# Attention layer on one core: root operations two to a step, normalisations in one slot, joints of the stages

## What is computed

```
h = _L0_tok_ref(log_dt, x, B, inv_A_real, A_imag, 1024)      # (16, 128, 1024)
h = jnp.concatenate([h, txt], axis=1)                         # (16, 205, 1024)
h = h + _L0_attn_ref(_layernorm(h, axis=-1), Wqkv, Wo)
h = h + _L0_ffn_ref(_layernorm(h, axis=-1), base_W, base_b, router_W, router_b, A, B, expert_map)
```

## Time and profile before

| | |
|---|---|
| median of 3 timed executions | 1586.72 us (1586.7 to 1587.28) |
| profiled execution | 1590.28 us, of which the span from first to last instruction 1588.5 us |
| busy: TensorE | 1454.7 us (92% of the span) |
| busy: VectorE | 1119.1 us (70%) |
| busy: ScalarE | 743.7 us (47%) |
| busy: GpSimd | 402.1 us (25%) |
| first stage | to 154 us |
| second stage | 154 to 924 us |
| third stage | 924 us to the end |
| pairs of the second stage, by their first projection product (L733) | start at 170.13, 229.40, 318.94, 408.43, 497.97, 587.50, 677.04 and 766.53 us; the tail begins at about 852.5 us |

### The profile page before, as it was taken

How to read it: one execution, slowest core, us unless ns; L and a number is a source line. 1 busy time by engine, 2 the same in 40 slices (tenths; PEclk the granted TensorE clock), 3 DMA queues, 4 the chain that set the end, 5 groups by cost and what they waited for, 6 DMA issues and landing times. The chain is left out here.

```text
span 1588.5 us, 28828 instructions
## 1 busy us (share of the span) xinstructions
PE 1454.7 (92%) x9700; PEld 1302.3 (82%) x9700; DVE 1119.1 (70%) x4187; ACT 743.7 (47%) x2642; POOL 402.1 (25%) x289
## 2 busy tenths in 40 slices
PE   0475899999999999999998979999999999999999
PEld 0475888888888788888887769999999999999888
DVE  8999689898988989898988755444444444444464
ACT  3595287887878687887887531111111111111101
POOL 0000154444445354444444400101010000000010
PEclk9988899999999999999999999999999999999999
DMA  9846555465636455465666251212121212121211
GB/s 293 280 99 139 99 81 114 65 128 85 121 59 120 85 81 116 66 129 80 132 149 120 88 198 40 80 40 79 40 79 40 79 40 79 40 79 40 70 49 41
DMA packets 107501, 152.51 MB, mean 96 GB/s; under 512 B 9060, under 2 KB 93412, under 8 KB 106456
## 3 DMA queue, kind: packets, MB, share of 16 engines
q1 hardware_dynamic: 105752, 150.27, 40.9%
q10 hardware_dynamic: 1632, 0.79, 0.3%
HBM read 73.90 MB, written 51.38 MB: 79 GB/s over the span
## 5 line engine op out<-in xcount | busy, mean ns | idle before, releaser
L828 ACT ACTIVATE P<-P,nmax 128x128 f32<-128x128 f32 (+1 forms) x1024 | 434.3, 426 | 95.2 <-DVE nmax L926 91.7
L899 POOL TENSOR_TENSOR P<-P,rden 128x512 f32<-128x512 f32 (+1 forms) x256 | 331.8, 1318 | 402.9 <-DVE rden L932 402.6
L926 DVE CUSTOM_DVE_ANT_0 P<-sc,mask 128x128 f32<-128x128 f32 (+1 forms) x1024 | 292.4, 323 | 71.3 <-PE sc L703 66.4
L733 PE MATMUL pr<-xT_hi,wq_hi 128*128 128x410 f32 x576 | 242.7, 421 | 0.7 <-DVE xT_lo L953 0.7
L938 DVE COPY PTR<-pt 128x282 f32<-128x282 f32 x512 | 221.1, 432 | 16.5 <-PE pt L713 15.4
L1202 PE MATMUL b<-w_hi,x2T_hi 128*128 128x390 f32 (+3 forms) x624 | 214.4, 344 | 1.0 <-DVE x2T_lo L1334 1.0
L1202 PE MATMUL b<-w_lo,x2T_hi 128*128 128x390 f32 (+3 forms) x624 | 212.5, 341 | 0.0
L1202 PE MATMUL b<-w_hi,x2T_lo 128*128 128x390 f32 (+3 forms) x624 | 212.0, 340 | 0.0
L1295 POOL TENSOR_TENSOR ht<-ht 128x1024 f32<-128x1024 f32 (+1 forms) x24 | 58.1, 2420 | 575.2 <-DVE ht L1324 575.2
L733 PE MATMUL pr<-xT_lo,wq_hi 128*128 128x410 f32 x576 | 201.3, 349 | 0.0
L733 PE MATMUL pr<-xT_hi,wq_lo 128*128 128x410 f32 x576 | 200.3, 348 | 0.0
(11 more groups left out here) (196 smaller groups left out, 2936.6 us busy)
## 6 DMA issues: line engine op xcount, KB each, us to landing
Qs<-q_hi SPq DMA_DIRECT2D x128, 205.0 KB, 4.8
ht<-h_dram SPq DMA_DIRECT2D x42, 512.0 KB, 3.6
Qs<-q_lo SPq DMA_DIRECT2D x64, 205.0 KB, 5.7
att_dram<-att SPq DMA_DIRECT2D x64, 205.0 KB, 2.9
at<-att_dram SPq DMA_DIRECT2D x25, 512.0 KB, 4.9
out<-ht SPq DMA_DIRECT2D x23, 512.0 KB, 2.6
h_dram<-Y SPq DMA_DIRECT2D x58, 128.0 KB, 3.1
h_dram<-in_txt SPq DMA_DIRECT2D x1, 4928.0 KB, 37.8
```

Of the source, the lines that this page charges most:

```text
L733: last = nc.tensor.matmul(out, w[a][:, i, cols], xT[x][:, i, :], start=(i == 0 and m == 0), stop=(i == KC - 1 and m == 2))
L828: last = nc.scalar.activation(P[rows, j % 2, i, cols], P[rows, j % 2, i, cols], ACT.Exp, scale=-1.0, bias=nmax[at], accum_out=den[at])
L899: lastp = nc.gpsimd.tensor_tensor(w, w, r, ALU.mult)
L926: lastv = v.tensor_tensor_reduce(P[0:n, j % 2, i, cols], sc[i % 2][0:n, cols], mask[0:n, m], 1.0, 3.0e38, ALU.add, ALU.min, nmax[0:n, j % ...
```

## The change

VectorE, next pair's normalisation: the eleven small operations lie two in a step (steps 26 to 31) and no longer one (26 to 36); the four row normalisations lie in steps 32, 34, 36 and 38, all in slot 4, and no longer in 38 to 41. End of the first stage: of the last step's eight stores five are issued by SP and three by ScalarE's queue, where it was two and six. Tail of the second stage: the two halves of the last weight piece are split at steps 76 and 79 (lo halves at 78 and 81) and no longer at 73 and 75 (75 and 77). Start of the third stage: the first tile's attention rows are split in two halves on ScalarE and VectorE, and TensorE begins with the first.

```diff
-    SP_LAST = 2
+    SP_LAST = 5
...
-    SPLIT_AT = [... for h in range(2)] + [GH * SLOTS + 1, GH * SLOTS + 3]
+    SPLIT_AT = [... for h in range(2)] + [GH * SLOTS + 4, GH * SLOTS + 7]
...
-        STATS_AT, RSTD_RATE = 14, 1
-        APPLY_AT, APPLY_EVERY = 38, 1
+        STATS_AT, RSTD_RATE = 14, 2
+        APPLY_AT, APPLY_EVERY = 32, 2
...
+    first_hi, first_lo = sem("first_hi"), sem("first_lo")
...
             def attn_out(t, par, n, between=None):
                 a = [w[:, par] for w in aT]
-                pe.wait_ge(a_lo, t + 1)
+                first = isinstance(t, int) and t == 0
+                if first:
+                    pe.wait_ge(first_lo, 1)
+                else:
+                    pe.wait_ge(a_lo, t + 1)
                 wait_count(pe, wo_read, t)
-                three(wo_ps[0], n, a, wo, slice(0, 512), KC)
+                three(wo_ps[0], n, a, wo, slice(0, 512), KC, between=(lambda: pe.wait_ge(a_lo, 1)) if first else None)
...
+            def a_first(half, done):
+                k = slice(half * KC // 2, (half + 1) * KC // 2)
+                nc.scalar.activation(aT[0][:, 0, k, :], at[:, 0, k, :], ACT.Copy).then_inc(done, 1)
...
-            a_split(0, 0, 0, 128)
+            act.wait_ge(a_loaded[0], 16)
+            a_first(0, first_hi)
+            a_first(1, a_hi)
...
+            def lo_first(half, ready, done):
+                k = slice(half * KC // 2, (half + 1) * KC // 2)
+                dve.wait_ge(ready, 1)
+                v.tensor_tensor(aT[1][:, 0, k, :], at[:, 0, k, :], aT[0][:, 0, k, :].bitcast(F32), ALU.subtract).then_inc(done, 1)
...
-            att_lo(0, 0, 128)
+            lo_first(0, first_hi, first_lo)
+            lo_first(1, a_hi, a_lo)
```

More of the change, by code:

```diff
@@ L538, in attention_block @@
     WO_RING = 4
-    SPLIT_AT = [GH * (n + 1) + 4 + 3 * h for n in range(WO_PIECES - 1) for h in range(2)] + [GH * SLOTS + 1, GH * SLOTS + 3]
+    SPLIT_AT = [GH * (n + 1) + 4 + 3 * h for n in range(WO_PIECES - 1) for h in range(2)] + [GH * SLOTS + 4, GH * SLOTS + 7]
     LO_AFTER = 2
```

## The result

The changed kernel takes 1592.46 us (median of 16 executions, 1590.51 to 1595.06), the kernel before 1588.83 us in 16 executions beside it (1586.7 to 1590.89). The ratio is 1.0023, its 95% interval 1.0016 to 1.0029: slower by 3.6 us (2.5 to 4.6). The profiled execution took 1592.99 us, its span 1591.2; before it was 1590.28 and 1588.5, so the two traces differ by 2.7 us, and that is what can be followed in them.

A forecast was written before the change was run, and what follows sets the result against it. VectorE, without room in slot 3 and held by GpSimd's instructions, was taken as the bound. Loop +10.7, tail -4.2, stores -0.7, third stage 0 make +5.8 us on a 1586.7 us median: 1592.5 us, range 1579 to 1600.

The forecast's parts named there:

- Bound by VectorE in slot 3: Slot 3 of a pair: VectorE, busy 9.99 of 10.5 us, has no room; slots 4 and 5 have 1.9 and 1.6 us.
- Follower waits for a whole GpSimd instruction: Steps 27 and 30: one root operation of about 1.5 us each, waiting out GpSimd; over 4 us summed per pair.
- GpSimd hands over kindly: Rival, loop: VectorE's waiting operation and its follower both pass before GpSimd's second instruction; -7.4 us, 1579.3 us, chance 0.17.
- Third normalisation waits 0.9 us: Slot 4, step 36: the normalisation waits 0.9 us for GpSimd; TensorE's transposes wait to 280.1, slot 5 begins 2.9 us later.
- My value for the case that it doesn't wait: Loop: if the normalisation didn't wait for GpSimd, 0.9 us per pair fall away, +5.3 instead of +10.7 us; ruled out.
- Slot 5 gives back 1.0 us: Slot 5: two normalisations gone, with TensorE's 0.74 us wait and some 0.25 us of delay before it: 1.0 us.
- First pair: Pair 0: no GpSimd work in slots 0 to 4, so it only gains 0.7 us in slot 5.
- The loop together: All pairs: +1.9 us for each of six, +11.4, less the first pair's 0.7: +10.7 us.
- Tail: Second stage's tail: TensorE starts 2.0 us earlier and the clock probably stays, 2.2 to 2.4 more: -4.2; -2.0 if it falls.
- Stores: First stage's end: stores issued earlier, -0.7 us; ends 0 if DMA engines limit, -2.6 if the issue does.
- Third stage: Its start: TensorE starts about 1.0 us earlier, but its second tile waits for the residual, cover 0.24 us: 0.
- The smaller loss: Rival, loop: normalisations don't wait or TensorE's slack takes more; +0.8 us per pair, about -1 in all, 1586, chance 0.17.

The follow-up runs named there:

- kernel 4: The changed kernel with root operations doubled in steps 26, 29, 32, 33, 34, where GpSimd is idle, and normalisations in steps 36 to 39: 1575.73 us, ratio 0.992.
- kernel 5: The kernel before with GpSimd multiplying one column per head instead of all, so its instructions are short: 1579.54 us, ratio 0.9941.
- kernel 6: The changed kernel with GpSimd multiplying one column per head instead of all, so its instructions are short: 1577.1 us, ratio 0.9921.
- kernel 8: The kernel before with two root operations in step 27 and none in step 28, the others one per step: 1594.8 us, ratio 1.0034.
- kernel 1: The changed kernel with only VectorE's new order; stores, tail splits and third stage's first tile as before: 1595.78 us, ratio 1.0042.
- kernel 3: The kernel before with only the root operations two per step; normalisations, stores, tail and third stage as before: 1594.23 us, ratio 1.0035.
- kernel 2: The kernel before with only the edits of stores, tail splits and third stage's first tile, VectorE's order as before: 1586.5 us, ratio 0.999.
- kernel 7: kernel 4 with the last three weight pieces in the tail split at steps 76, 78, 80 instead of 71, 76, 79: 1574.55 us, ratio 0.9908.

## Why the prediction was right, and where it was not

The direction and the mechanism were right and the time, 1592.5, was met within 0.1 us; but that is luck, errors and the base cancelling. Forecast was +5.8 us, measured +3.6 by the medians and +2.7 between the two traces. Against the forecast the loop of pairs lost 5.0 us less and the stretch before it gained 0.9 us more, while the tail gained 2.3 us less and the third stage lost 0.5 us: 5.8 - 5.0 - 0.9 + 2.3 + 0.5 = 2.7. And the three executions on which the sum stood lay 2.1 us below the median of all 16.

- **Bound by VectorE in slot 3: right.** 12.04 of 12.21 us busy, and TensorE waits for its copies only.
- **Follower waits for a whole GpSimd instruction: right, shown.** The root operations of a pair add up to 4.29 us, as foretold over 4 (before they took 3.12, not the 2.9 of the prediction). One operation of 1.5 us each in steps 27 and 30, as forecast; kernels 4, 5, 6 and 8 put it on and off. The walked copies of steps 27, 28, 30 and 31 were 267.7, 268.8, 272.7 and 273.6; with the 2.76 us the trace has 267.5, 268.6, 272.3 and 273.2. The rule of the Trainium skill ("SBUF — State Buffer", Who interferes with whom), that an operation with two inputs in SBUF contends with a GpSimd instruction that reads SBUF, agrees with these runs: 1.48 us beside GpSimd's long instruction, 0.17 without it. The rival that GpSimd hands over kindly fell: the follower missed the change-over in every doubled step that lay on it.
- **Third normalisation waits 0.9 us: the step that failed.** It took 1.00 us instead of 0.80, a wait of 0.2 us where the sum had 0.9. Three things made up the difference. The walk had GpSimd's third pair end at 278.9; with the 2.76 us it ended at 278.3, as the normalisation in step 34 ran 0.4 us earlier than walked. GpSimd was then held less by it: its pair starts at 272.53, with the normalisation on VectorE until 273.13, and takes 3.02 us, 0.44 longer than the other two. And the waiting normalisation was let in some 0.24 us before GpSimd's recorded end: 275.11 + 1.00 less its own 0.80 is 275.31, and GpSimd ends at 275.55. (VectorE came to it 0.1 us earlier than walked, which goes the other way.) So TensorE's waits in slot 4 are 0.32 and 0.32 us where I had it waiting to 280.1, and slot 5 begins 2.1 us late instead of 2.9. A pair lost 1.15 us and not 1.9. My value for the case that it doesn't wait, +5.3 for the loop, is nearly what came, +5.7: that the normalisation would wait was right, but to rule out the smaller value for it was not, since how long it waits hangs on when it arrives. The lesson of the step is that a wait taken from the end of a long walk carries the error of all its steps: 0.4 us of walk was over half of the 0.7 us.
- **Slot 5 gives back 1.0 us: right** (0.96). **First pair:** -1.2 for -0.7. I had read off one wait; slot 6 gave 0.1 and slot 5 the rest, 1.1. **The loop together:** 6.9 - 1.2 = +5.7 where +10.7 was forecast.
- **Tail: the wait right, the clock wrong.** The timelines of TensorE and VectorE around the first output product:

```profile
860.09 0.33 PE L711 MATMUL pt<-ident,P 128*128 128x128 f32 x1 [1.16 <-DVE PTR L938]
...
861.71 0.45 PE L711 MATMUL pt<-ident,P 128*128 128x128 f32 x1 [0.69 <-DVE PTR L938]
...
862.98 0.79 PE L795 MATMUL pr<-wq_hi,xT_hi 128*128 128x512 f32 x1 [0.56 <-DVE xT_lo L942]
...
861.98 0.94 DVE L942 TENSOR_TENSOR xT_lo<-at,xT_hi 128x512 fp32r<-128x512 f32 x1
```

and two windows of it (granted clock third from last):

```profile
860.96:867.79 6.83, 5.58 (x21) 4.73 (x21) 4.89 (x25) 4.38 (x20) 5.06 (x4) 0.50 0.82 128
858.00:860.96 2.96, 1.74 (x11) 1.15 (x10) 2.91 (x12) 2.96 (x11) 0.00 (x0) 1.00 1.10 136
```

The tile's operation takes 0.94 us instead of 2.04, the wait is 0.56 for 2.79, and the product starts 6.2 us into the tail instead of 8.1: the 2.0 us of the forecast. But I had laid the half clock on the one long wait. It is granted at 0.50 (the 1.2 GHz level) from 860.96 on, before that wait, after 2.96 us at full clock in which TensorE was busy 1.74. The matmul at 861.71 already shows it (0.45 us for the 0.33 of the one at 860.09). In the trace before, too, the fall did not come behind the wait but 0.7 us into it, at 858.67, and lasted the same 6.83 us; the prediction's window began at 860.70 and does not show that:

```profile
858.67:865.50 6.83, 4.72 (x17) 4.15 (x18) 5.49 (x20) 2.85 (x11) 2.85 (x3) 0.50 0.53 67
```

So the shorter wait did not bring the clock back, and the tail's term was -1.9, the end that I had stated for that case, and not -4.2. What in TensorE's work before 860.96 decides it these runs do not settle: kernel 4 has the tail of the changed kernel, and the clock was half for 3.4 us of it and not 6.8. That most of the long wait was GpSimd's, kernel 5 shows: with the order of before and GpSimd short it is 0.91 us and not 2.79.

- **Stores: no gain shown.** The timelines of SP's queue (the load behind the stores) and of VectorE:

```profile
151.59 0.84 SPq L224 DMA_DIRECT2D ht<-h_dram  x2
...
151.60 1.53 DVE L416 TENSOR_SCALAR ht<-ht,tab 77x1024 f32<-77x1024 f32 x2
...
155.13 1.29 DVE L983 BATCH_NORM_STATS2 stats<-ht 128x6 f32<-128x512 f32 x2 [0.67 <-DMA ht<-h_dram]
```

The load behind the stores is issued 1.4 us earlier, of which 0.8 us is that the last step already began earlier. From ScalarE's first store of that step to the load it is 8.4 us, and 9.0 before. But with the split of before kernels 1, 3, 5 and 8 have 8.4, 8.3, 7.5 and 8.4, and with the new one kernels 2, 4, 6 and 7 have 8.4, 6.9, 8.4 and 8.3. Pair 0 starts at 167.9 to 170.1 us in the five traces with the split of before, the kernel before being the latest, and at 167.5 to 169.3 in the five with the new one. So the -1.6 us of the table is not to be told from scatter, and the forecast of -0.7 is neither shown nor refuted. What can be read is that VectorE, as I had put it for the case of a large gain, now ends last: its normalisation of the text ends at 153.13 and the next stage starts at 153.64. That holds nothing up: the statistics behind it still wait 0.67 us for the load. The Trainium skill ("DMA: Bandwidth & Descriptors", Issuing engines are not separate DMA queues) has spreading save issue time alone; these intervals don't decide between that and a gain of 0.6 us.

- **Third stage: right.** TensorE starts 5.28 us after the tail where it was 6.23. Its second tile, which waits for the residual of tile 0 as before, starts 21.1 us after the tail, where it was 21.2. That wait is 2.19 us and was 1.80, so it was more than the 0.24 us of cover that the prediction read off, and the earlier start could bring nothing. (It grew by 0.4 us only, since the first tile's product ran 0.5 us longer: 4.84 us of it at a granted clock of 0.50 where it was 3.87.) The stretch behind the tail is 0.5 us longer, within the 667.6 to 669.1 us of the ten traces. TensorE's timeline, and behind it the second tile's line of before:

```profile
927.80 0.80 PE L1203 MATMUL wo<-wq_hi,aT_hi 128*128 128x512 f32 x1 [5.28 <-DVE aT_lo L1340]
...
943.65 0.47 PE L1203 MATMUL wo<-wq_hi,aT_hi 128*128 128x512 f32 x1 [2.19 <-DVE ht L1326]
```

```profile
941.49 0.48 PE L1202 MATMUL wo<-wq_hi,aT_hi 128*128 128x512 f32 x1 [1.80 <-DVE ht L1315]
```

- **No rival came.** The clock is 1.00 in slots 3 to 5. The smaller loss was the nearest of them: its mechanism (the normalisation hardly waits) holds for slot 4, though the time, 1586, doesn't, since the base was higher and the tail gave less than it took for granted.

## What to carry to other kernels

Before doubling short dependent operations in a step, lay them beside the other engine's instructions on the shared resource: what counts is not their 0.15 us but whether the second still starts before the next instruction there, and if not it costs that whole instruction (1.5 us here). The same eleven operations and four normalisations cost 1.15 us a pair in one order and gained 1.8 in another, which puts the doubled steps where GpSimd is idle or has yet to start, so look for idle stretches of GpSimd rather than of VectorE. Do not add a return of the clock to a shortened wait unless a trace shows at which work the clock fell.

## What was not expected of the hardware

- VectorE is let in before the end that the trace gives for GpSimd's instruction: a normalisation by some 0.24 us (275.31 and 275.55), as far as the recorded end is exact.
- The contention goes both ways: beside a normalisation already running on VectorE GpSimd's pair took 3.02 us for 2.58 (272.53), and in kernel 6 0.81 for 0.36. In the tail, before and after, GpSimd's second instruction took 2.0 us for 1.56 beside a lo half on VectorE.
- TensorE's granted clock was 0.50 for 6.8 us of the tail before and after and in kernels 2, 3, 5, 7 and 8, for 10.2 us in kernel 1 and for 3.4 in kernels 4 and 6, while the wait at the output projection's first product was 0.56 us after and in kernel 2, 0.82 in kernel 4, 2.52 in kernel 1 and 2.79 before.
